# Attention in a decoder layer: softmax sums from ScalarE beside the first score pass, their logarithm in the stacked exponent row, and no denominator matmuls

## The reference

```python
x = x + self_attention(layernorm(x))           # causal
x = x + cross_attention(layernorm(x), ctx)     # keys masked by a padding mask
x = x + moe(layernorm(x))                      # 8 experts, top 1
# an attention: scores = q k^T / sqrt(32), masked; probs = softmax(scores); out = (probs v) W_o + b_o
```

## Time and profile before

| | us |
|---|---|
| median of 3 runs | 1946.59 (1946.36 to 1949.47) |
| the profiled execution, its own time | 1945.76 |
| its span, first to last instruction | 1944.2 |
| PE busy | 1858.7 |
| DVE busy | 1336.1 |
| ACT busy | 1121.2 |
| POOL busy | 958.8 |
| mean granted clock of TensorE | 0.981 |

### The profile page before, as it was taken

One profiled execution on the slowest core, in us unless ns is written; L12 is line 12 of the kernel. 1 busy time (PEld: TensorE's weight loads), 2 busy tenths in 40 slices (PEclk: granted clock), 3 DMA queues, 4 the chain that ended last, 5 costly groups with the idle time before them and its releaser, 6 DMA issues. The chain is left out here.

```text
span 1944.2 us, 34701 instructions
## 1 busy us (share of the span) xinstructions
PE 1858.7 (96%) x10902; PEld 1311.2 (67%) x10902; DVE 1336.1 (69%) x2835; ACT 1121.2 (58%) x2156; POOL 958.8 (49%) x1162
## 2 busy tenths in 40 slices
PE   6999999999999999999999999999999976899997
PEld 4667777777777766656666666666666535799996
DVE  5667666676767676767575766666676548688886
ACT  3555555555555565656565655555565434788885
POOL 3445545554555455544455554545554434454442
PEclk9999999999999999999999999999999987899999
DMA  5554554556455574445445354534443517843231
GB/s 170 133 148 112 134 130 106 136 113 144 99 120 124 133 183 122 104 123 131 109 120 118 83 126 94 140 89 115 105 106 79 120 55 262 319 140 89 82 82 28
DMA packets 135160, 239.60 MB, mean 123 GB/s; under 512 B 29963, under 2 KB 31283, under 8 KB 134929
## 3 DMA queue, kind: packets, MB, share of 16 engines
q1 hardware_dynamic: 105392, 184.46, 34.8%
q0 software_dynamic: 22192, 51.66, 13.4%
q10 hardware_dynamic: 7408, 1.42, 0.4%
HBM read 112.99 MB, written 47.40 MB: 82 GB/s over the span
## 5 line engine op out<-in xcount | busy, mean ns | idle before, releaser
L559 ACT ACTIVATE attn_probs<-attn_sT 128x512 f32<-128x512 f32 (+3 forms) x1024 | 528.8, 518 | 475.2 <-PE attn_sT L873 472.0
L467 POOL TENSOR_TENSOR attn_probs<-attn_probs 128x512 f32<-128x512 f32 (+2 forms) x384 | 530.9, 1401 | 180.0 <-PE attn_o_ps L888 131.6
L668 DVE TENSOR_REDUCE attn_m_col<-attn_sS 128x1 f32<-128x512 f32 x512 | 342.6, 687 | 194.9 <-PE attn_sS L857 187.2
L873 PE MATMUL attn_sT<-attn_stack 98*128 98x512 f32 (+2 forms) x1024 | 386.9, 389 | 0.3 <-ACT attn_probs L559 0.3
L857 PE MATMUL attn_sS<-attn_stack 97*128 97x512 f32 (+2 forms) x1024 | 369.7, 371 | 14.0 <-DVE attn_m_col L668 3.4
L674 DVE CUSTOM_DVE_ANT_0 attn_sS<-attn_sS,attn_cT_low 128x128 f32<-128x128 f32 x496 | 240.9, 504 | 172.5 <-PE attn_sS L857 169.0
L873 PEld LDWEIGHTS attn_sT<-attn_stack 98*128 98x128 f32 x1024 | 188.0, 188 | 206.0 <-ACT attn_probs L559 128.6
L455 POOL TENSOR_SCALAR_AFFINE_SELECT attn_probs<-attn_probs 128x256 f32<-128x256 f32 x256 | 119.5, 467 | 347.3 <-ACT attn_probs L559 347.3
L857 PEld LDWEIGHTS attn_sS<-attn_stack 97*128 97x128 f32 x1024 | 194.2, 190 | 69.9 <-DVE attn_m_col L668 15.6
L888 PE MATMUL attn_o_ps<-attn_probs,attn_V 128*32 128x512 f32 (+3 forms) x2048 | 233.6, 527 | 4.9 <-ACT attn_probs L559 2.0
L837 PE MATMUL attn_pj<-attn_xT_high,attn_w_high 128*128 128x512 f32 x384 | 154.8, 403 | 1.4 <-DVE attn_xT_low L652 1.4
(11 more groups left out here) (227 smaller groups left out, 3645.1 us busy)
## 6 DMA issues: line engine op xcount, KB each, us to landing
attn_stack<-attn_stage SPq DMA_DIRECT2D x666, 128.0 KB, 2.3
attn_rows<-in_x_dram SPq DMA_DIRECT2D x64, 256.0 KB, 4.3
attn_rows<-x_after_self SPq DMA_DIRECT2D x64, 256.0 KB, 4.3
moe_w<-in_L_ffn_W_dram SPq DMA_DIRECT2D x16, 1024.0 KB, 15.5
attn_stack<-attn_stage POOLq DMA_DIRECT2D x96, 128.0 KB, 3.3
x_after_self<-attn_rows SPq DMA_DIRECT2D x32, 256.0 KB, 2.6
x_after_self<-in_L_attn_b_dense_dram POOLq DMA_DIRECT2D x32, 256.0 KB, 4.9
attn_rows<-in_ctx_dram SPq DMA_DIRECT2D x32, 256.0 KB, 3.1
```

The lines of the kernel that those rows point to most:

```text
L467: pool.tensor_tensor(total, total, tile_of(n, kb)[:, js, q0:S], ALU.add).then_inc(added, 1)
L559: act.activation(tile_of(n, kb)[:, j, q0:S], sT[:, i % 2, q0:S], ACT.Exp, scale=SCALE).then_inc(exp_done, 1)
L668: dve.tensor_reduce(to, sS[:, k % 2], AX_X, ALU.max).then_inc(s_free, 1)
L873: pe.matmul(sT[:, i % 2, q0:S], stack[0:ROW_MAX + 1, n % 2, 1, j, kb * P:(kb + 1) * P], stack[0:ROW_MAX + 1, n % 2, 0, j, q0:S], start=Tru ...
```

## The change

The denominators are computed in the first pass. DVE's row operation is now a multiply with -SCALE, an addition of the mask and a minimum, in place in the PSUM bank (also in the cross layers, with a mask of zeros); it is L665 in the changed kernel. ScalarE then takes the exponential of the bank in place, with the row's minimum as bias, and sums the row by its accumulator output (`sum_row`, L561). At step 12 it takes Ln and Exp of the 16 sums of each row (L566, L570), DVE computes minus (maximum plus logarithm, refined once) in high and low part in five small operations (`lse`, L673 to L681), PE turns them at step 13 (`lse_row`, L852), DVE copies them out (`copy_lse`), and SP writes them as two rows of `stack` (L422), where ScalarE's queue wrote one. The second pass then yields normalized probabilities, and `add_probs`, `sums`, the two large Ln and Exp, the copy of `o_ps` and the three products on DVE are gone; high and low part of the output come straight from `o_ps`, at steps 0 and 1. The three banks `sS` (two and the former `extra`) form one ring for scores, turned rows and the turned logarithms; a bank of scores is free once ScalarE has summed it. The scores of the first pass are spread differently (`N_SCORES`), and one is issued a step earlier, at step 15 of the group before. Copies of v go from ScalarE to DVE, the normalization of rows from ScalarE to GpSimd (but for the first batch), and the output ring has 6 places, not 5.

```diff
-    N_SCORES = (2, 1, 1, 2, 1, 1, 2, 1, 1, 2, 1, 1, 0, 0, 0, 0)
+    N_SCORES = (2, 1, 1, 1, 1, 1, 2, 1, 2, 1, 1, 1, 0, 0, 0, 1)
+    AHEAD = 1
...
     def scores_of(n, q):
+        if q == Q - 1:
+            return [(n + 2, 0, i) for i in range(AHEAD)] if in_groups(n + 2) else []
...
-    RING = len(shares[True])
+    RING, BANKS = len(shares[True]), 3
...
-        extra = ps("extra", [P, S])
-        sS = ps("sS", [P, 2, S])
+        sS = ps("sS", [P, BANKS, S])
...
+        def ring_taken(eng, key):
+            if key[0] == "mT":
+                eng.wait_ge(lse_copied, key[1] + 1)
+            elif key[0] in ("x", "c"):
+                eng.wait_ge(turned_free, turned_at[key] + 1)
             else:
+                eng.wait_ge(summed_row, score_at[key] + 1)
...
                 if j >= 0 and in_groups(m) and not (is_cross(m) and j == POOL_HEAD) and not (m == 0 and j % 2):
                     wait_to_stack(sp, m, j)
                     stack_head(sp, m, j)
+                if q == 14 and in_groups(n + 1):
+                    sp.wait_ge(lse_copied, n + 2)
+                    sp.dma_start(stack_f32[ROW_LSE:ROW_LSE + 2, (n + 1) % 2, 0].rearrange("o j s -> o (j s)"),
+                                 lse_rows[:].bitcast(F32)).then_inc(lse_stacked, 16)
...
-            def add_probs(n, kb, j0, j1):
...
+            def normalize(b, t):
+                to = row_block(("x", b, t))
+                pool.wait_ge(ln_ready, 4 * (2 * b + t // 2 + 1))
+                pool.tensor_scalar(to, to, rstd[:, t:t + 1], nmr[:, t:t + 1], ALU.mult, ALU.add).then_inc(xn_ready, 1)
...
+            def sum_row(key):
+                m, j, qb = key
+                act.wait_ge(measured_max, score_at[key] + 1)
+                at = bank_of(key)[:, 0:width_of(m, qb)]
...
+                act.activation(at, at, ACT.Exp, scale=-1.0, bias=m_col[:, column(*key)],
+                               accum_out=sum_col[:, column(*key)]).then_inc(summed_row, 1)
+
+            def log_of_sums(m):
+                act.wait_ge(summed_row, Q * (m + 1))
+                act.activation(log_col[:], sum_col[:], ACT.Ln).then_inc(logged, 1)
+
+            def inverse_of_sums(m):
+                act.wait_ge(logged, 2 * m + 1)
+                act.activation(inv_col[:], log_col[:], ACT.Exp, scale=-1.0).then_inc(logged, 1)
+
+            def high_of_output(n):
                 act.wait_ge(pv_done, NB * (n + 1))
...
-                act.activation(oT[0][:, n % ORING], o_sb[:], ACT.Identity,
+                act.activation(oT[0][:, n % ORING], o_ps[:], ACT.Identity,
                                bias=bias_of(n, 2)).then_inc(oT_high, 1)
...
+                dve.tensor_tensor_reduce(at, at, mask, -SCALE, LARGEST, ALU.add, ALU.min,
+                                         m_col[:, column(*key)]).then_inc(measured_max, 1)
+
+            def lse(m):
+                at = 5 * m
+                dve.wait_ge(logged, 2 * m + 2)
...
+                dve.tensor_tensor(m_col[:], m_col[:], log_col[:], ALU.subtract).then_inc(lse_ready, 1)
+                dve.tensor_tensor(sum_col[:], sum_col[:], inv_col[:], ALU.mult).then_inc(lse_ready, 1)
+                dve.wait_ge(lse_ready, at + 2)
+                dve.scalar_tensor_tensor(out=m_col[:], in0=sum_col[:], scalar=-1.0, in1=m_col[:],
+                                         op0=ALU.add, op1=ALU.subtract).then_inc(lse_ready, 1)
+                dve.wait_ge(lse_ready, at + 3)
+                dve.tensor_scalar(lse_col[:, 0], m_col[:], -1.0 / SCALE, None, ALU.mult).then_inc(lse_ready, 1)
+                dve.wait_ge(lse_ready, at + 4)
+                dve.scalar_tensor_tensor(out=lse_col[:, 1], in0=m_col[:], scalar=-1.0 / SCALE, in1=lse_col[:, 0].bitcast(F32),
+                                         op0=ALU.mult, op1=ALU.subtract).then_inc(lse_ready, 1)
+
+            def copy_lse(m):
+                wait_turned(dve, ("mT", m))
...
+                dve.tensor_copy(lse_rows[:], bank_of(("mT", m))[0:2 * Q, 0:P]).then_inc(lse_copied, 1)
...
+            def lse_row(m):
                 key = ("mT", m)
-                begin_aux(key)
-                pe.wait_ge(s_free, s_at[m, J - 1, NB - 1] + 1)
-                pe.transpose(extra[0:Q, 0:P], m_col[:, m % 2], ident[:]).then_inc(aux_full, 1)
+                begin(key)
+                pe.wait_ge(lse_ready, 5 * (m + 1))
+                pe.transpose(bank_of(key)[0:2 * Q, 0:P], lse_col[:].bitcast(F32).rearrange("p a i -> p (a i)"),
+                             ident[:]).then_inc(ring_full, 1)
...
                 if kb == 0 and j == 0:
-                    pe.wait_ge(max_stacked, 16 * (n + 1))
+                    pe.wait_ge(lse_stacked, 16 * (n + 1))
...
-            def sums(n):
...
-                        if q == 0:
-                            sums(of)
```

290 lines of the change are left out of this document (112 added, 178 removed).

## The result

The changed kernel takes **2223.67 us** (median of 4 runs) against 1946.74: a ratio of 1.1434 with a 95% interval of 1.1392 to 1.1475, 277 us slower. The prediction was 2000 us, with a range of 1925 to 2050. Its sign was right, its size fell far outside the range. The profiled execution's span is 2221.2 us, against 1944.2.

A forecast was written before the change was run, and what follows sets the result against it. TensorE was taken to bound both attentions. Self groups +46 us, cross groups +13 and the end -5 gave +54 on the profiled 1945.76: 2000 us, likeliest range 1970 to 2035, eight in ten 1925 to 2050.

The forecast's parts named there:

- TensorE bounds the kernel before, 90 us go out: Both attentions: removed `sums` matmuls save 1.1 us a self group, 1.7 a cross group, 90 us over 32 groups each.
- The row in SP's queue: Group's end: row issued behind three heads lands late; ordinary self groups +1.9 us before banks, turning ones about 0.
- the term "7.4 us": Masked cross groups: time that three heads hold SP before the row can be issued, 7.4 us.
- The term "2.3 us": Row's DMA: landing 2.3 us after its issue, the median of the earlier write of the maxima.
- The forecast of +59 us for both layers: Growth over eight batches: about +46 us in self groups and +13 us in cross groups.
- The stall at `lse_row`: Step 13: PE waits 1.0 us for a 4.2 to 4.3 us chain, costing extra only in unmasked cross groups.
- ScalarE's price: ScalarE's added sums: 0.67 us each, from 0.68 for the exponential and 0.19 for the read, less overlaps.
- ScalarE's effect: First second-pass matmul to SP's start, cross group: 16.0 of 16.65 us; late banks 0.5 us, self 0.2 to 0.3.
- The turning groups: Groups that turn rows: about 0 in self layers, a gain of 0.7 us each in cross layers.
- Rival 1: ScalarE becomes the bound, at 0.87 us a sum, deciding from 0.72: 2050 us, chance 0.18.
- Rivals 2 and 3: Row in SP's queue not late, about 1928 us, chance 0.14; neither wait bites, 1850 us, chance 0.06.
- The gain of 5 us at the end: Last group's end: PE's idle 5.05 us and 1.8 of `sums` give way to 1.5 us, -5 us.

The follow-up runs named there:

- e4c: Kernel before without its 8 denominator products a group, one transpose of 16 columns in their place, outputs undivided: 1874.86 us, ratio 0.9632.
- e6: Kernel before with its row of maxima issued from SP's queue behind three heads instead of ScalarE's queue: 2074.56 us, ratio 1.0651.
- e10: e9 with TensorE's row matmul at step 13 moved behind the three matmuls of the step's second part: 2015.83 us, ratio 1.0349.
- e5: e1 with each exponential with a sum cut to one column, output not the reference's: 1944.7 us, ratio 0.9991.
- e15: e14 with the row matmul at the very end of step 13, behind the value matmuls: 1934.21 us, ratio 0.9945.
- e12: e10 with each step's sums of the step before put ahead of the step's exponential on ScalarE: 1983.3 us, ratio 1.0198.
- e9: e1 with the next group's scores spread otherwise over the steps, only in groups that turn context rows: 2061.08 us, ratio 1.0585.
- e14: e12 with value matmuls of the first three key blocks one step later and projection chunks in their place: 1997.28 us, ratio 1.0266.
- e1: Changed kernel with the DMA of the two logarithm rows issued from ScalarE's queue at step 14 instead of SP's: 2088.86 us, ratio 1.0728.
- e7: Changed kernel with filler matmuls (10 or 5, none after turning groups) while TensorE would wait for the row's DMA: 2193.17 us, ratio 1.1277.
- e2: Changed kernel with each exponential with a sum cut to one column, output not the reference's: 2152.39 us, ratio 1.1058.

## Why the prediction was wrong, step by step

- **TensorE bounds the kernel before, 90 us go out: right.** Without the products 72 us are saved (e4c), the full amount in cross groups, a little over half in self groups.
- **The row in SP's queue: mechanism and place right, size too small.** For the ordinary self group 1.9 us was forecast and 2.2 is what e6 shows, for the turning one 0 and 0.1. In masked cross groups the term "7.4 us" failed: SP took 8.4 us in e6 and 8.0 in the changed kernel. The term "2.3 us" held for the masked groups of e6 and failed elsewhere: 4.1 us in e6's groups without masks, and 3.8 us from issue to matmul in the masked groups of the changed kernel. Why the row is late there isn't shown; busy DMA engines alone are not it. The first and last self batch had no term of their own. The forecast of +59 us for both layers (with banks and stall) stands against 129 in e6, with half clock.
- **The stall at `lse_row`: 1.0 us forecast, 1.14 us in the rows above.** The chain from the last score to the row matmul was told as 4.2 to 4.3 us and is 5.0 in cross groups, 4.0 in self groups. The prediction let it lie beside the longer wait for the row and cost nothing more there. No run tests that with the row in SP's queue; with the row on ScalarE's, e10 shows a gain of 45 us when the row matmul comes later.
- **ScalarE's price: right. ScalarE's effect: the step that failed.** 0.66 us a sum against 0.67. But the prediction added up ScalarE's work from a group's start to SP's start (16.0 of 16.65 us), concluded "it just keeps up", and took 0.25 to 0.5 us a group for late banks, under 20 us in the whole sum. e5 puts the time of the sums at 144 us once the queue is out of the way. A sum of work was the wrong test: the budget was not exceeded, as e15 shows with the same work in a kernel slightly faster than before. What costs, in the cross groups above all, is the work at its place in a fixed order: each sum stands behind an exponential that waits for a matmul of its own step, and a score waits for a sum three banks back. Putting the sums ahead (e12) gave 32 us by itself. Four changes of order (e9, e10, e12 and e14 with e15), on ScalarE and on TensorE, gave 155 us on top of e1.
- **The turning groups: no price given.** They were forecast to gain 0.7 us in cross layers and lost 7.3. The four context blocks, which were turned into `extra` before, now use the scores' three banks too: 25 uses in 16 steps, where by my reading two neighbouring steps may have three. e9 gives back 3.1 us of it.
- **The half clock: not in the sum at all.** 249 us in place of 74. e7 shows about 0.4 us of time for each microsecond of it, so some 70 us.
- **The rivals.** Rival 1 (ScalarE) named the right engine with the wrong condition: it was to decide from 0.72 us a sum and decides at 0.66. Rivals 2 and 3 took the waits for absorbed, which e1 and e6 exclude. The gain of 5 us at the end came: from the start of the last group to the end it is 366.8 us in place of 375.3, and PE's last wait for the output's low part is 1.6 us in place of 5.05.

Of the 277 us, then: about 135 by the queue, with its half clock (e1); 28, 45 and 32 by banks in turning groups, the place of the row matmul, and the sums' place behind exponentials (e9, e10, e12); and 38 more, net of the 72 to 90 us that the products' removal gives, which moving values and row matmul turned into a gain of 10 us (e15). The contributions depend on the order in which they are taken, as e2 and e5 show.

## What to carry to other kernels

When work moves to an engine that has room, follow one buffer round its ring, instruction by instruction, before trusting the engine's sum of work: who waits in the same step for what, and behind which instruction does the release stand. A small DMA that the next phase waits for belongs on a queue where nothing large is ahead of it, and its landing should be forecast with its spread and not by a median from another queue. And where TensorE was never idle, every forecast of a new wait should carry a surcharge for the clock that the wait takes away: here some 70 us beside 234 us of waits.
